# VectorE's residual additions of step 4, moved behind the maximum of that step (and in one chunk behind the queries' low part too), in an fp32 attention and expert kernel

## The reference

```python
x = x + attention(layernorm(x), ctx_512, Wq, Wkv_expand, Wout)   # 16 heads of 32, causal, softmax
x = x + ffn(layernorm(x), router_w, router_b, expert_w, expert_b) # 8 experts, top 2 per output column
```

## Time and profile before

| what | us |
| --- | --- |
| median of 3 runs | 1930.66 (1930.08 to 1932.46) |
| the profiled execution | 1928.12 |
| its span, first to last instruction | 1926.4 |
| PE busy | 1894.4 (98%) |
| DVE busy | 1424.0 (74%) |
| ACT busy | 1044.6 (54%) |
| residuals on line 1584 | first at 130.4, last at 574.7 |

### The profile page before, as it was taken

One profiled execution on the slowest core, in us unless ns is written; L12 is line 12 of the kernel. 1 busy time (PEld: TensorE's weight loads), 2 busy tenths in 40 slices (PEclk: granted clock), 3 DMA queues, 4 the chain that ended last, 5 costly groups with the idle time before them and its releaser, 6 DMA issues.

```text
span 1926.4 us, 30339 instructions
## 1 busy us (share of the span) xinstructions
PE 1894.4 (98%) x9748; PEld 1501.9 (78%) x9748; DVE 1424.0 (74%) x2824; ACT 1044.6 (54%) x2070; POOL 849.8 (44%) x1022
## 2 busy tenths in 40 slices
PE   7999999999999999999999999999999999999999
PEld 6667776777667888888888888788888888888887
DVE  6767767767769478879788888577777777777752
ACT  5666656566554357787787777533334443333330
POOL 6877777777672236536445435011122211111110
PEclk9999999999999999999999999999999999999999
DMA  7554555455467677778656556722223322222210
GB/s 210 124 142 127 139 154 126 131 155 127 118 188 265 192 247 249 268 228 273 201 202 224 189 198 220 268 91 82 82 82 101 117 87 82 84 97 86 82 44 33
DMA packets 104558, 294.56 MB, mean 153 GB/s; under 512 B 13873, under 2 KB 15921, under 8 KB 99346
## 3 DMA queue, kind: packets, MB, share of 16 engines
q1 hardware_dynamic: 92378, 209.63, 34.0%
q10 hardware_dynamic: 8760, 67.19, 10.5%
q0 software_dynamic: 3328, 16.78, 3.6%
HBM read 150.31 MB, written 109.16 MB: 135 GB/s over the span
## 4 chain that ended last, share of the span: by engine, by line
PE 89%; DVE 4%; DMA 2%; issue 2%; ACT 2%; SPq 1%; ACTq 0%; DVEq 0%
PE pair L283 22%; PE pair L285 22%; PE pair L284 22%; PE pair L773 4%; PE ps L790 3%; PE pair L734 3%; PE ps L283 3%; PE ps L284 3%; PE ps L285 3%; PE ps L810 1%; DVE pair L1556 1%; DVE nmax L1550 1%; SPq L406 1%; PE ps L1015 1%; ACT pT L1249 1%
## 5 line engine op out<-in xcount | busy, mean ns | idle before, releaser
L283 PE MATMUL pair<-w_h,hT 128*128 128x512 f32 x1912 | 747.4, 391 | 0.7 <-DVE xb L1879 0.4
L285 PE MATMUL pair<-w_h,hT 128*128 128x512 f32 x1912 | 744.3, 389 | 0.0
L284 PE MATMUL pair<-w_l,hT 128*128 128x512 f32 x1912 | 744.1, 389 | 0.0
L2077 POOL TENSOR_TENSOR logits<-logits,second 128x512 f32<-128x512 f32 x224 | 298.5, 1370 | 595.8 <-DVE second L1774 595.5
L283 PEld LDWEIGHTS pair<-w_h,hT 128*128 128x128 f32 x1912 | 358.9, 188 | 76.4 <-issue 2.0
L285 PEld LDWEIGHTS pair<-w_h,hT 128*128 128x128 f32 x1912 | 358.9, 188 | 75.2
L284 PEld LDWEIGHTS pair<-w_l,hT 128*128 128x128 f32 x1912 | 359.0, 188 | 73.4
L1879 DVE SCALAR_TENSOR_TENSOR xb<-pair,c_all,xb 128x512 f32<-128x512 f32 x256 | 191.9, 750 | 179.3 <-PE pair L285 174.1
L1249 ACT ACTIVATE pT<-pair,zero 128x1024 f32<-128x1024 f32 (+3 forms) x256 | 202.7, 792 | 188.9 <-PE pair L773 179.9
L1556 DVE CUSTOM_DVE_ANT_0 pair<-pair,future 128x384 f32<-128x384 f32 (+1 forms) x330 | 180.1, 558 | 115.8 <-PE pair L734 111.9
L1354 ACT ACTIVATE w<-tree 128x512 f32<-128x512 f32 x32 | 20.2, 632 | 384.7 <-DVE tree L1776 384.7
(11 more groups left out here) (206 smaller groups left out, 2627.2 us busy)
## 6 DMA issues: line engine op xcount, KB each, us to landing
logits<-lg_all ACTq DMA_DIRECT2D x32, 1792.0 KB, 8.6
qk_st<-qk SPq DMA_DIRECT2D x366, 128.0 KB, 2.5
lg_all<-ev_a SPq DMA_DIRECT2D x30, 768.0 KB, 8.7
lg_all<-ev_b SPq DMA_DIRECT2D x29, 768.0 KB, 3.9
xb<-x SPq DMA_DIRECT2D x64, 256.0 KB, 4.2
hT_all<-hT SPq DMA_DIRECT2D x32, 512.0 KB, 4.4
hT<-hT_all SPq DMA_DIRECT2D x32, 512.0 KB, 3.9
w_fix<-in_expertT POOLq DMA_DIRECT2D x8, 1024.0 KB, 5.7
```

What stands on the lines that cost most here:

```text
L283: pe.matmul(dst, lh, rh, start=start, stop=False)
L284: pe.matmul(dst, lh, rl, start=False, stop=False)
L285: return pe.matmul(dst, ll, rh, start=False, stop=stop)
L2077: pool.tensor_tensor(logits[t % 2][:, e - 1, :], logits[t % 2][:, e - 1, :], second[:], ALU.subtract)\
```

## The change

Nothing of the computation changes. VectorE's list is reordered in step 4 of chunks 1 and 3 of batches 1 to 6: twelve places. In chunk 3 the residual comes directly behind the maximum (1579, 1550, 1584, 1535). In chunk 1 it comes behind the maximum and the queries' low part (1579, 1550, 1535, 1584). In all other steps the residual stays where it was. The order of TensorE, ScalarE, GpSimd and SP is the same as before.

```diff
-                        i = None if first else summed_block(c, v, last)
-                        if i is not None:
-                            residual(b - 1, i, out_bank(i, last))
+                        done = None if first else summed_block(c, v, last)
+                        if done is not None and v != SCALED:
+                            residual(b - 1, done, out_bank(done, last))
...
                         if more or c + g < KC:
                             maxima(n + g, (c + g) % KC, vv, masked(c, v, last))
+                        if done is not None and v == SCALED and c == KC - 1:
+                            residual(b - 1, done, out_bank(done, last))
                         if QUERY.get(v) == KC - 1 and ahead:
                             lo_of(n + AHEAD, QL, "q", j_ps[1])
+                        if done is not None and v == SCALED and c < KC - 1:
+                            residual(b - 1, done, out_bank(done, last))
```

## The result

The changed kernel takes 1935.61 us (median of 13 runs, 1933.35 to 1940.01) against 1930.67 for the kernel before in as many. The ratio is 1.0027, with a 95% interval of 1.002 to 1.0034: slower by 5.2 us (3.9 to 6.6), by 4.9 between the two medians. The prediction was 1935.2.

What follows compares the result with a forecast made beforehand. TensorE, busy 98% of the span, was taken to bound the kernel, with two gates per chunk. Chunk 3's +2.0 and chunk 1's +2.5 us make +4.5: 1930.66 becomes 1935.2 us, range 1932.0 to 1938.2.

Steps and rivals of the forecast that it cites:

- The first gate: Step 4's reduction (line 1550) and the transposition of the maxima (line 752), twelve places: 0.26 us earlier each, 3.1 us if kept.
- VectorE's idle time: VectorE idles 0.34 us (bounds 0 and 0.43) before line 1550, and everything behind the three operations is later by that.
- The order on VectorE is free: Rival, 5%: only the idle 0.34 us slows chunk 3; without it chunk 3 costs 0 and the time is 1931.1 us.
- Chunk 3, +2.0: Six places: VectorE's 0.34 us passes through line 1565 and the rows' landing to line 773, costing 2.0 us in all.
- Chunk 1, +2.5: Six places: residual and SP's store, load and rows move 1.27 us, so line 773 waits; 0.41 us each, 2.5 in all.
- The other terms: After both waits no later stretch takes the loss back; the profiled execution goes from 1928.1 to 1932.6 us.
- The first gate decides: Rival, 7%: VectorE's order does not reach the rows, the twelve places gain 0.26 us each; 1927.5 us, or 1925.6.
- The room in chunk 1 suffices: Rival, 20%: SP's list moves by less than its 1.15 us of room, chunk 1 costs nothing; 1932.7 us, or 1931.1.
- More than the rows: Rival, 10%: chunk 1's output projection in step 6 waits for the residual's bank, adding 2.0 us; 1937.2 us.
- the signs to look for: In the profile after, among others: line 773 waits for `nm_l` in all twelve places, not 6, some 6 us in all.

Runs made afterwards that it cites:

- e1_chunk3_only: The changed kernel with chunk 1's residual back in its old place, so only chunk 3 is changed; 1933.07 us, ratio 1.0010 to the kernel before.
- e6_low_late: The kernel before, with chunk 3's low part of the queries made in step 7 instead of step 4; 1929.64 us, ratio 0.9997 to the kernel before.
- e3_rows_first: The changed kernel, with SP issuing chunk 1's two rows ahead of the load into the stored tile; 1930.88 us, ratio 1.0002 to the kernel before.
- e4_old_rows_first: The kernel before, with SP issuing chunk 1's two rows ahead of the load into the stored tile; 1929.88 us, ratio 0.9999 to the kernel before.
- e2_chunk1_only: The changed kernel with chunk 3's residual back in its old place, so only chunk 1 is changed; 1933.17 us, ratio 1.0017 to the kernel before.
- e5_chunk1_second: The kernel before, with only chunk 1's residual moved, behind the maximum but ahead of the queries' low part; 1933.29 us, ratio 1.0017 to the kernel before.

## Why the prediction came out, point by point

**The first gate.** Predicted 0.26 us earlier, the wait under 0.2; measured 0.24 earlier in batch 3 (from line 739 to line 752 it is 1.00 us where it was 1.24), with 0.18 left of 0.42. Shown by the timeline.

**VectorE's idle time.** Predicted 0.34 us, with bounds of 0 and 0.43; line 1550 stands 0.44 us behind line 739, and line 1565 is 0.35 later in chunk 3 and 0.39 in chunk 1. (The bracket says 0.27 or 0.26, as it counts from the end that the row shows for the operation ahead, and that overlaps the next by 0.08.) The rival that the order is free is out, by e1_chunk3_only.

**Chunk 3, +2.0.** Measured +1.9, and +2.1 alone. Here the prediction named one of two gates that move together. It said that the rows, and not TensorE, start the next chunk, but TensorE also waits 0.30 us in step 6 for the maximum of line 1556, which is later by the same 0.34, and comes to line 773 with only 0.03 to 0.04 us to spare in batches 1 to 4. In the kernel before it was 0.01 to 0.05, so it is open there too which of the two held, and the earlier trace rows can't tell them apart. The size is right either way, which is luck as far as the reason given goes. Which of the two would hold if the other were gone was not tried apart: e6_low_late moves both.

**Chunk 1, +2.5.** Measured +2.6, 2.0 in chunk 1 and 0.6 in chunk 2, where the weights that are loaded behind the landing belong: 0.10 a batch against the 0.11 of the working. The residual's move is 1.31 us where 1.27 was predicted. That the load ahead of the rows in SP's list is the cause is shown by e3_rows_first, and that the rows had room before by e4_old_rows_first. The landings scatter the single places: TensorE's waits in the six batches are 0.17, 0.72, 0.24, 0.10, 0.57 and 0.60 us. So the agreement of the sum is closer than the method: the same change alone came to 2.1 in e2_chunk1_only. The two places that the prediction averaged are not the loosest and the tightest, either: from the row's issue to line 773 it is 3.17 us in batches 4 and 5, above the 3.15 of batch 3. The same sum over all six, each with its own landing, gives 0.44 us a batch instead of 0.41. And VectorE had less room than the working says: it compared line 1565's start with the rows' issue at 275.55, but its end, 275.42, is only 0.13 us ahead of it, and in e3_rows_first the issue comes 0.08 us behind that end. It did no harm, as SP's list was later by more.

**The other terms.** No later stretch took the loss back, as predicted. The profiled execution was foretold at 1932.6 and took 1935.15; 1.5 us of the difference is the landing in batch 0 that is shown above, which the forecast could not know.

**The rivals.** "The first gate decides" is out, by the total and by both halves. "The room in chunk 1 suffices" failed in all six places, by 0.10 us of TensorE's time in the loosest (batch 4). "The order on VectorE is free" is out, as said. "More than the rows" did not come: the projection behind the keys waits for nothing at 278.13 (batch 3), since the residual had ended at 277.70.

**What was wrong in the signs to look for.** Line 773 does wait twelve times for `nm_l`, but not in the twelve places: six are behind chunk 1, two behind chunk 3 (batches 5 and 6), and four belong to batches 0 and 7. Of the six waits before none was behind chunk 1, two were behind chunk 3 (batches 5 and 6 again) and four in batches 0 and 7, so they were not a count of the chunk 3 places. Behind chunk 3 of batches 1 to 4 line 773 starts 0.12 us behind the row's landing in both kernels, with TensorE's last work ending within 0.05 us of it, and the trace puts no wait for the row there. For the same reason the sum of 9.0 us on the weights' side says little; the idle time of TensorE itself in the six places of chunk 1 is 2.4 us.

## What to carry to other kernels

An operation that fills a wait is free where it stands. Moved behind the wait, it leaves the wait empty, and what stands behind all of them in the list is later by that length (0.34 us here); it costs time where another engine waits for something in that part of the list, and what has passed ahead of the operation gains. Before an operation is moved, list what hangs on its semaphore in every queue, the DMA issuer's too: a wait for a store's landing ahead of an urgent row has a slack, and the move spends it. And a gain at one gate is worth what the next gates let through, so they are best opened together, with runs that show what each does alone.

## What the runs showed that was not expected

A quarter of a microsecond a batch in chunk 3 uncovered a gate on GpSimd, which is busy 44% of the span and had not been waited for at line 810: it takes back 1.7 us in six batches. From the end of the queries' low part to the keys' projection that waits for it 0.24 us pass (277.24 to 277.48 in e5_chunk1_second), which no busy row shows. The landing of the 8 KB row takes 1.9 us in most places, up to 2.5 with a load issued just ahead of it, and 3.4 us in batch 0 of the changed kernel's profile: 1.5 us of TensorE's time that no change of order explains.
